# A four-layer kernel on one Trainium2 core: the value matmuls of the first attention in bursts of four units instead of two

## The chip, the cores and the metric

The kernel runs on one core of a Trainium2 chip. A core has TensorE (PE, with its weight loads PEld), VectorE (DVE), ScalarE (ACT), GpSimd (POOL) and SyncE (SP, which issues DMAs), each with its own instruction stream, tied by semaphores. The metric is the device time of one execution in microseconds, lower is better.

## What is computed

Four layers in sequence, each followed by a layer norm over the residual sum. The change lies in the first, an attention over two sequences of 2048 tokens with 16 heads of 16 columns; a decay multiplies the scores before the softmax. The other three are a feed-forward layer with weights and inputs rounded to a 4-bit grid, a causal linear attention, and a mixture of eight experts.

```python
def _L0_attn_ref(x, Wq, bq, Wk, bk, Wv, bv, Wo, bo, alpha):
    ...
    scores = jnp.einsum('bqhd,bkhd->bhqk', q, k) * scale
    idx = jnp.arange(T)
    lag = jnp.abs(idx[:, None] - idx[None, :]).astype(jnp.float32)
    decay = jnp.exp(-alpha * lag * DT)
    scores = scores * decay
    attn = jax.nn.softmax(scores, axis=-1)
    out = jnp.einsum('bhqk,bkhd->bqhd', attn, v).reshape(B, T, D)
    return out @ Wo.T + bo
```

## The kernel before

The first attention works on 16 pairs of heads in sequence. For each pair there are two kinds of work.

The **units**. A unit is one block of 128 keys against 512 queries, for both heads of the pair; a query block has 16 units (TB) and a pair has four query blocks, so 64 units (UNITS). PE makes the unit's scores (line 823, two matmuls, 512 columns) into one of two PSUM buffers `ps_s`. ACT makes the exponentials from there into `prob` (line 969), a ring of RING units in SBUF. Four of the 16 units of a query block are diagonal ("d" in SCORE_ORDER): ACT copies their scores to `tb` (line 959), POOL multiplies them by the decay (line 927) and subtracts the row's maximum (line 930), and ACT takes the exponential from `tb` (line 966), four to nine units later, as EXP_ORDER says. In the last pair DVE does POOL's part (lines 883 and 887). The values (line 839) multiply `prob` by V into `ps_o`: four groups of 32 columns of the array work side by side, and each matmul shows as two records in the trace, so a unit has eight records. Each query block sums in its own half of `ps_o`; behind its last unit ACT copies the half to `ot` (line 946), PE transposes it (line 846) and DVE divides (lines 904 and 906): a "sum".

The **tiles**. For the pair after this one, 128 tiles of approximate scores (line 799, one matmul of 512 columns each) give the rows' maxima. PE writes a tile into one of three PSUM banks of the ring `ps_r` (BANKS), and DVE multiplies it by the decay and takes its maximum (line 870, two records: the pass and the reading of the accumulator, which releases the bank). The sums and the turn of the maxima take a slot in the same ring. Once per pair DVE folds the maxima (line 891), PE transposes them (line 804), and DVE splits them into three parts (lines 331 to 339): the "turn".

The order on PE is written out by `body_steps`, and DVE follows the same list: two units, each with its two tiles around it, then the values of the two units that lie LAG = 4 units back, then the next two units. EARLY shifts the tiles three ahead, so three of them stand in a row where a pair begins. ACT has its own loop over the exponentials (EXP_ORDER), with the copies to `tb` in front of some and the copy of the last query block's sums behind the second exponential of each query block. The semaphores that matter: `ring_free` (DVE has read a bank; PE waits for the user of the same bank, three slots earlier as a rule), `exp` and `copied` (a score buffer is free; PE waits for the score two before), `value` (the values of a unit are done; ACT waits for the unit RING before, and the copy out for the whole block), `evac` (the sums are copied; PE waits before it begins the next block but one in that half).

Of the kernel before, what the change touches and what calls it, by code (L numbers as in the profile page):

```python
# [19 lines left out]
TB = T // P  # L20
# [75 lines left out]
def up_to(n):  # L96

    return n + 1
# [32 lines left out]
UNITS = QB * TB  # L131
# [4 lines left out]
TURN = 3  # L136
BANKS = 3
EARLY = 3
RING = 6
LAG = 4  # L140
EXP0, PV0, EV0 = TB, 5, 1

# [19 lines left out]
def e_unit(u):  # L164
    return unit(EXP_ORDER, u)


def place_in(order, u, other):

    qb, n = divmod(u, TB)  # L170
    nth = order[:n].count(order[n])
    return qb * TB + [i for i, c in enumerate(other) if c == order[n]][nth]


def diag_count(u):

    qb, n = divmod(u, TB)
    return qb * TPC + SCORE_ORDER[:n].count("d")


def body_kind(this, nxt):

    if not this:
        return "first"
    if not this.back():
        return "lead"
    return "last" if not nxt else "mid" if nxt.more() else "late"


@lru_cache(None)  # L190
def body_steps(kind):

    fold, turn = [("fold", None, 1)], [("turn", None, 1)]
    if kind == "first":
        small = [("tile", t, 1) for t in range(TILES)] + fold + [("tile", t, 2) for t in range(TURN)] + turn
        small += [("tile", t, 2) for t in range(TURN, SKEW)]
        steps, slot = [], 0
        for what, n, ahead in small:  # L200
            steps.append((what, n, slot if what != "fold" else None, ahead))
            slot += what != "fold"
        return steps
    small = []
    if kind != "last":
        small = [("tile", t, 1) for t in range(SKEW, TILES)] + fold
        if kind in ("lead", "mid"):
            small += [("tile", t, 2) for t in range(TURN)] + turn + [("tile", t, 2) for t in range(TURN, SKEW)]
        else:
            small += turn  # L210
    steps, done, slot = [], 0, 0
    def next_small(upto):
        nonlocal done, slot
        while done < min(len(small), upto):
            what, n, ahead = small[done]
            steps.append((what, n, slot if what != "fold" else None, ahead))
            done, slot = done + 1, slot + (what != "fold")

    for two in range(0, UNITS + (LAG if kind == "last" else 0), 2):
        for u in (two, two + 1):  # L220
            next_small(EARLY + 2 * u)
            if u < UNITS:
                steps.append(("score", u, None, 0))
            next_small(EARLY + 2 * u + 1)
        if two >= LAG:
            steps.append(("values", two - LAG, None, 0))
        elif kind != "lead":
            steps.append(("values", UNITS + two - LAG, None, -1))
        if two % TB == TB // 2 and (two > TB or kind != "lead"):
            steps.append(("sum", two // TB - 1 if two > TB else QB - 1, slot, 0 if two > TB else -1))  # L230
            slot += 1
    assert done == len(small)
    if kind == "last":
        steps.append(("sum", QB - 1, slot, 0))
    return steps


def slot_of(kind, what, n, ahead=None):

    return next(slot for w, m, slot, far in body_steps(kind) if (w, m) == (what, n) and ahead in (None, far))  # L240


@lru_cache(None)
def ring_use(kind):


    users = [-3, -2, -1]
    if kind == "last":
        past = ring_use("late")
        for i, (bank, _) in enumerate(past):  # L250
            users[bank] = i - len(past)
    out, bank = [], 1 if kind == "first" else 0
    for what, n, slot, _ in body_steps(kind):
        if slot is None:
            continue
        if kind != "lead" and what == "sum" and n in (0, QB - 1):
            bank = (bank + 1) % BANKS
        out.append((bank, slot - users[bank]))
        users[bank] = slot
        bank = (bank + 1) % BANKS  # L260
    if kind in ("first", "lead", "mid"):
        assert [b for b, _ in out[-3:]] == [0, 1, 2]
    return out
# [420 lines left out]
def stage_attention(nc, g, a, p1, p2, vp0, mx):  # L684
    with ExitStack() as ctx:
# [4 lines left out]
        mb = ctx.enter_context(nc.sbuf_tensor("mb", [P, 2, 2, T], F32))  # L690
        prob = ctx.enter_context(nc.sbuf_tensor("prob", [P, RING, 2, CH], F32))
        tb = ctx.enter_context(nc.sbuf_tensor("tb", [P, DIAGS, 2, CH], F32))
# [10 lines left out]
        def walk(body):  # L703

            def run(eng):
                body(eng, None, Pair(0, 0))
                for c in range(PAIRS - 1):
                    body(eng, Pair(0, c), Pair(0, c + 1))
                body(eng, Pair(0, PAIRS - 1), None)
            return run  # L710

        def first_slot(this):
            if not this:
                return 0
            if not this.back():
                return FIRST
            return this.times(SLOTS) + (FIRST - 1 if this.more() else FIRST - 1 - SKEW)

        with nc.Block() as block:
# [63 lines left out]
            def _(pe):  # L783
                def body(_, this, nxt):
                    if this is None:
                        return
                    for kind, n, slot, ahead in body_steps(body_kind(this, nxt)):
# [38 lines left out]
                        elif kind == "values":  # L826
# [6 lines left out]
                            for m in (n, n + 1):  # L833
                                qb, kb, _ = e_unit(m)
                                for f in range(2):
                                    for hh in range(2):
                                        q = 2 * f + hh
                                        out = ps_o[32 * q:32 * q + VW, qb % 2, :]
                                        mm = pe.matmul(out.rearrange("p (j c) -> p j c", c=P), vp[whose.par][:, kb, hh, :],  # L839
                                                       prob[:, m % RING, hh, :].rearrange("p (j f c) -> p f j c", f=2, c=P)[:, f],  # L840
                                                       start=(m % TB == 0), stop=(m % TB == TB - 1), skip_group_check=True)
# [93 lines left out]
            @block.scalar  # L935
            def _(act):
                def body(_, this, nxt):
                    if this is None:
                        return
                    slots = {n + QB * far: slot for k, n, slot, far in body_steps(body_kind(this, nxt)) if k == "sum"}  # L940

                    def evacuate(qb):
                        act.wait_ge(s["value"], up_to(this.times(UNITS) + (qb + 1) * TB + PV0))

                        act.wait_ge(s["ring_full"], up_to(first_slot(this) + (slots[qb - 1] + 1 if qb - 1 in slots else 0)))
                        act.activation(ot[:], ps_o[:, qb % 2, :], ACT.Copy).then_inc(s["evac"], 1)

                    e_diags = [n for n in range(UNITS) if e_unit(n)[2]]
                    for n in range(UNITS):
                        qb, kb, diag = e_unit(n)  # L950
                        if not diag:
                            mine = place_in(EXP_ORDER, n, SCORE_ORDER)
                            if SCORE_ORDER[(mine - 1) % TB] == "d" and nxt:

                                k = diag_count(mine - 1)
                                act.wait_ge(s["score"], up_to(this.times(UNITS) + mine))

                                act.wait_ge(s["exp"], up_to(this.times(UNITS) + place_in(SCORE_ORDER, mine - 1, EXP_ORDER) - TB + 1 + EXP0))
                                act.activation(tb[:, k % DIAGS], ps_s[:, (mine - 1) % 2], ACT.Copy).then_inc(s["copied"], 1)  # L959

                        last = UNITS % RING if n < UNITS % RING else RING
                        act.wait_ge(s["value"], up_to(this.times(UNITS) + n - last + 1 + PV0))
                        if diag:
                            k = e_diags.index(n)
                            act.wait_ge(s["less"], up_to(this.times(TB) + k + 1))
                            act.activation(prob[:, n % RING], tb[:, k % DIAGS], ACT.Exp).then_inc(s["exp"], 1)  # L966
                        else:
                            act.wait_ge(s["score"], up_to(this.times(UNITS) + mine + 1))
                            act.activation(prob[:, n % RING], ps_s[:, mine % 2], ACT.Exp,  # L969
                                           scale=csc[:, qb * TB + kb:qb * TB + kb + 1]).then_inc(s["exp"], 1)  # L970
                        if n % TB == 1 and (n > TB or this.back()):
                            evacuate(n // TB - 1)
                    if not nxt:
                        evacuate(QB - 1)

                walk(body)(act)


# [1606 lines left out]
```

## Time and profile before

| | |
|---|---|
| median of 3 runs | 3417.16 us (3413.48 to 3422.5) |
| the profiled execution, its own time | 3417.1 us |
| its span, first to last instruction | 3415.3 us |
| mean granted TensorE clock | 0.95 |
| busy, share of the span | PE 90%, PEld 51%, DVE 71%, ACT 53%, POOL 42% |
| records of L839 (values) | 8192, from 291.3 to 1785.7 us |
| records of L799 (tiles), attention alone | 1894 |

The first attention runs from about 290 to 1788 us. What is ahead of it is its projections, and what is behind it the other three layers. Busy shares are averages over stages with different limits, so for this change the rows of the attention alone are to be read.

### The profile page before, as it was taken

The numbers are of one execution on the slowest core, as the hardware profiler recorded it, in microseconds if no ns is written. First come the engines' busy times: TensorE is split into PE (matmuls) and PEld (weight loads), VectorE is DVE, ScalarE is ACT, GpSimd is POOL, SyncE is SP. The second block draws the span as 40 slices with busy tenths as digits, with TensorE's granted clock in tenths as the row PEclk, the third lists the DMA queues.
The fourth block names the chain that finished last, engine by engine and source line by source line (L and its number), as shares of the span: only waits on it lengthen the run. The fifth ranks groups of instructions, "written<-read, shape, count | busy, mean of one in ns | idle before, by whom it ended". The sixth has DMA issues, their size and how long they took to land. (4 is left out here: it accounts for less than half of the span.)

```text
span 3415.3 us, 66017 instructions
## 1 busy us (share of the span) xinstructions
PE 3071.1 (90%) x22948; PEld 1734.7 (51%) x22949; DVE 2440.1 (71%) x6509; ACT 1802.2 (53%) x2255; POOL 1422.7 (42%) x741
## 2 busy tenths in 40 slices
PE   3678999999999999999985998989999987999996
PEld 1232333333333333333323565556666666999995
DVE  4679999999999999999747888844555554333334
ACT  4235888888888888888873333322222222111112
POOL 6346787878878787787801000000000111111110
PEclk7788999999999999999997999989899988999998
DMA  5575434332344443333204110030000005555555
GB/s 154 144 192 138 90 84 83 79 78 76 67 91 92 93 89 82 83 79 78 57 13 78 25 38 5 1 99 14 14 14 14 23 18 191 183 182 177 182 184 182
DMA packets 201698, 304.65 MB, mean 89 GB/s; under 512 B 86192, under 2 KB 150544, under 8 KB 199248
## 3 DMA queue, kind: packets, MB, share of 16 engines
q1 hardware_dynamic: 192640, 277.89, 31.6%
q0 software_dynamic: 7632, 22.16, 1.8%
q8 instruction: 159, 2.61, 0.3%
q14 instruction: 115, 0.94, 0.1%
q10 hardware_dynamic: 1152, 1.05, 0.1%
HBM read 238.91 MB, written 62.13 MB: 88 GB/s over the span
## 5 line engine op out<-in xcount | busy, mean ns | idle before, releaser
L870 DVE CUSTOM_DVE_ANT_0 ps_r<-ps_r,toep 128x512 f32<-128x512 f32 x1894 | 1252.3, 716 | 71.8 <-PE ps_r L799 31.6
L969 ACT ACTIVATE prob<-ps_s,csc 128x1024 f32<-128x1024 f32 x768 | 829.9, 1118 | 151.4 <-PE ps_s L823 129.6
L927 POOL TENSOR_TENSOR tb<-tb,toep 128x1024 f32<-128x1024 f32 x240 | 568.1, 2367 | 264.0 <-ACT tb L959 229.4
L799 PE MATMUL ps_r<-p 96*128 96x512 bf16 x1894 | 646.3, 382 | 10.1 <-DVE mp L870 4.1
L823 PE MATMUL ps_s<-p 120*128 120x512 bf16 (+1 forms) x2048 | 609.3, 380 | 27.1 <-ACT tb L959 16.4
L930 POOL TENSOR_TENSOR tb<-tb,mb 128x1024 f32<-128x1024 f32 x240 | 567.8, 2366 | 18.8
L839 PE MATMUL ps_o<-prob,vp 128*32 128x256 f32 x8192 | 548.2, 385 | 1.2 <-ACT prob L966 0.9
L799 PEld LDWEIGHTS ps_r<-p 96*128 96x128 bf16 x1894 | 181.4, 96 | 406.2 <-DVE mp L870 258.0
L1695 POOL DMA_INDIRECT slots_scratch<-l_xh,l_place x64 | 62.5, 976 | 710.3 <-DVE l_xh L2020 693.3
L839 PEld LDWEIGHTS ps_o<-prob,vp 128*32 128x32 f32 x8192 | 213.7, 109 | 269.6 <-issue 177.9
L823 PEld LDWEIGHTS ps_s<-p 120*128 120x128 bf16 (+1 forms) x2048 | 189.6, 98 | 237.2 <-ACT tb L959 46.6
L2335 ACT ACTIVATE e_aT<-e_u 128x1024 f32<-128x1024 f32 x71 | 75.0, 1057 | 421.4 <-DVE e_u L2406 421.4
L966 ACT ACTIVATE prob<-tb 128x1024 f32<-128x1024 f32 x256 | 272.3, 1064 | 2.9 <-POOL tb L930 2.8
L2281 PEld LDWEIGHTS ps_eu<-e_hT,moe_w 128*128 128x128 f32 x2272 | 266.3, 193 | 7.7 <-DVE e_hT L2397 4.1
L2281 PE MATMUL ps_eu<-e_hT,moe_w 128*128 128x128 f32 x2272 | 266.9, 276 | 3.5 <-DVE e_hT L2397 3.5
L870 DVE DVE_READ_ACCUMULATOR2_ANT mp<- 128x1 f32 x1894 | 266.2, 141 | 0.0
L959 ACT ACTIVATE tb<-ps_s 128x1024 f32<-128x1024 f32 x240 | 247.0, 1029 | 32.7 <-PE ps_s L823 31.3
L2374 POOL DMA_INDIRECT ytok_scratch<-e_y,e_name x71 | 69.2, 975 | 463.0 <-DVE e_y L2452 463.0
L2299 PE MATMUL ps_ed<-moe_w,e_aT 128*128 x1136 | 257.0, 379 | 0.8 <-DVE e_y L2452 0.8
L2406 DVE TENSOR_TENSOR e_u<-ps_eu,moe_cols 128x1024 f32<-128x1024 f32 x71 | 86.9, 1224 | 210.1 <-PE ps_eu L2281 210.1
L2299 PEld LDWEIGHTS ps_ed<-moe_w,e_aT 128*128 128x128 f32 x1136 | 210.3, 190 | 26.9 <-issue 1.2
L1280 PE MATMUL ps_du<-wgu,d_xs 128*128 128x512 f32 (+1 forms) x384 | 164.6, 580 | 4.2 <-DVE d_h L1559 2.6
(324 smaller groups left out, 3580.4 us busy)
## 6 DMA issues: line engine op xcount, KB each, us to landing
moe_w<-in_W_dram SPq DMA_DIRECT2D x79, 1024.0 KB, 5.3
p<-scr_scratch SPq DMA_DIRECT2D x288, 192.0 KB
mb<-mrow_scratch SPq DMA_DIRECT2D x16, 2048.0 KB, 7.4
scr_scratch<-part SPq DMA_DIRECT2D x64, 384.0 KB, 6.7
p<-scr_scratch SPq DMA_DIRECT2D x96, 128.0 KB
moe_pt<-slots_scratch SPq DMA_DIRECT2D x72, 132.0 KB, 2.1
vscr_scratch<-vsb SPq DMA_DIRECT2D x8, 1024.0 KB, 8.8
vp<-vscr_scratch SPq DMA_DIRECT2D x16, 512.0 KB, 22.2
```

The lines of the kernel that those rows point to most:

```text
L799: pe.matmul(ps_r[:, bank, :], buf[:, hh, 0, qt * P:(qt + 1) * P], buf[:, hh, 1, kc * CH:(kc + 1) * CH], start=True, stop=True)\
L823: mm = pe.matmul(ps_s[:, n % 2, hh, :], buf[0:rows, hh, KEY, kb * P:(kb + 1) * P], buf[0:rows, hh, var, qb * CH:(qb + 1) * CH], start=True ...
L839: mm = pe.matmul(out.rearrange("p (j c) -> p j c", c=P), vp[whose.par][:, kb, hh, :], prob[:, m % RING, hh, :].rearrange("p (j f c) -> p f ...
L870: dve.tensor_tensor_reduce(ps_r[:, bank, :], ps_r[:, bank, :], toep[:, col:col + CH], 1.0, -3.0e38, ALU.mult, ALU.max, mp[:, whose.par, hh ...
L927: pool.tensor_tensor(tb[:, k % DIAGS], tb[:, k % DIAGS], toep[:, col:col + CH].unsqueeze(1) .broadcast_to([P, 2, CH]), ALU.mult).then_inc( ...
L930: pool.tensor_tensor(tb[:, k % DIAGS], tb[:, k % DIAGS], mb[:, this.par, :, qb * CH:(qb + 1) * CH], ALU.add).then_inc(s["less"], 1)
L959: act.activation(tb[:, k % DIAGS], ps_s[:, (mine - 1) % 2], ACT.Copy).then_inc(s["copied"], 1)
L966: act.activation(prob[:, n % RING], tb[:, k % DIAGS], ACT.Exp).then_inc(s["exp"], 1)
L969: act.activation(prob[:, n % RING], ps_s[:, mine % 2], ACT.Exp, scale=csc[:, qb * TB + kb:qb * TB + kb + 1]).then_inc(s["exp"], 1)
L1280: mm = pe.matmul(ps_u[:, lo:hi], xs[:, c % 2, kc, t * P:(t + 1) * P], wgu[:, kc, lo:hi], start=(kc == 0), stop=(kc == KC - 1), skip_group_ ...
L2281: mm = pe.matmul(ps_u[:, tile.par, f, :], w1[:, tile.par, kc, f * P:(f + 1) * P], hT[:, kc, :], start=(kc == 0), stop=(kc == KC - 1), skip ...
L2299: mm = pe.matmul(ps_d[:, 0:D], aT[:, this.par, f, :], w["w2"][:, bass.ds(e, 1), f, :].rearrange("p a n -> p (a n)"), start=(f == 0), stop= ...
```

## The change

RING goes from 6 to 8 units. The values no longer come two units at a time behind every second score but four units at a time behind every fourth: behind scores 2 and 3 of each four (of the step with `two` = 2, 6, 10, ...) PE works off the units `two` - 6 to `two` - 3. The oldest two units are so read two units later than before, and the younger two at the same place. ACT copies a block's sums out behind the fourth exponential of the next block, not the second. PV0, a count of units ahead of the first one, follows RING.

```diff
-RING = 6
+RING = 8
 LAG = 4
-EXP0, PV0, EV0 = TB, 5, 1
+BURST = 4
+EXP0, PV0, EV0 = TB, RING - 1, 1
...
-        if two >= LAG:
-            steps.append(("values", two - LAG, None, 0))
-        elif kind != "lead":
-            steps.append(("values", UNITS + two - LAG, None, -1))
+        if (two - LAG) % BURST == BURST - 2 and (two >= LAG or kind != "lead"):
+            for n in range(two - LAG - BURST + 2, two - LAG + 2, 2):
+                steps.append(("values", n % UNITS, None, 0 if n >= 0 else -1))
         if two % TB == TB // 2 and (two > TB or kind != "lead"):
...
-                        if n % TB == 1 and (n > TB or this.back()):
+                        if n % TB == BURST - 1 and (n > TB or this.back()):
                             evacuate(n // TB - 1)
```

On PE, four units in the middle of a pair: `ps_r` are the tiles, `ps_s` the scores (two instructions each), `ps_o` the values, whose 8 instructions are two units and 16 records of the trace. Before:

```order
L839 MATMUL ps_o<-prob,vp 32x256 x8
L799 MATMUL ps_r<-p_0 128x512
L823 MATMUL ps_s<-p_1 128x512 x2
L799 MATMUL ps_r<-p_0 128x512 x2
L823 MATMUL ps_s<-p_1 128x512 x2
L799 MATMUL ps_r<-p_0 128x512
L839 MATMUL ps_o<-prob,vp 32x256 x8
```

and now:

```order
L839 MATMUL ps_o<-prob,vp 32x256 x16
L799 MATMUL ps_r<-p_0 128x512
L823 MATMUL ps_s<-p_1 128x512 x2
L799 MATMUL ps_r<-p_0 128x512 x2
L823 MATMUL ps_s<-p_1 128x512 x2
L799 MATMUL ps_r<-p_0 128x512 x2
L823 MATMUL ps_s<-p_1 128x512 x2
L799 MATMUL ps_r<-p_0 128x512 x2
L823 MATMUL ps_s<-p_1 128x512 x2
L799 MATMUL ps_r<-p_0 128x512
L839 MATMUL ps_o<-prob,vp 32x256 x16
```

Four tiles stood between two bursts, now eight do, and a burst is twice as long.

On ACT, where a query block begins: L959 copies diagonal scores, L969 and L966 are exponentials, L946 copies the last block's sums out. Before:

```order
L946 ACTIVATE ot<-ps_o 128x256
L959 ACTIVATE tb<-ps_s 128x1024
L969 ACTIVATE prob<-ps_s,csc 128x1024 x2
L966 ACTIVATE prob<-tb 128x1024
L969 ACTIVATE prob<-ps_s,csc 128x1024
```

and now:

```order
L959 ACTIVATE tb<-ps_s 128x1024
L969 ACTIVATE prob<-ps_s,csc 128x1024 x2
L946 ACTIVATE ot<-ps_o 128x256
L966 ACTIVATE prob<-tb 128x1024
L969 ACTIVATE prob<-ps_s,csc 128x1024
```

The copy out has moved behind a copy of scores and two exponentials. DVE, POOL and SP have the same instructions in the same order as before; the waits that count units of the ring moved with it.

## Rows read from the trace of the kernel before

**Rows 1.** The page: the span, and each engine's busy us, share and instructions.

```profile
span 3415.3 us, 66017 instructions
...
PE 3071.1 (90%) x22948; PEld 1734.7 (51%) x22949; DVE 2440.1 (71%) x6509; ACT 1802.2 (53%) x2255; POOL 1422.7 (42%) x741
```

**Rows 2.** Stretch table, and line 804's group (ns min/median/max, first and last start).

```profile
core 0: us, PE busy (x) PEld busy (x) DVE busy (x) ACT busy (x) POOL busy (x), PEclk, DMA share, GB/s
360.30:1689.40 1329.10, 1307.87 (x10861) 504.06 (x10857) 1254.59 (x3776) 1139.50 (x1176) 1057.85 (x448) 1.00 0.37 82
...
1689.40:1788.00 98.60, 84.81 (x823) 28.49 (x823) 43.41 (x49) 85.10 (x88) 17.37 (x8) 1.00 0.09 27
...
L804 PE MATMUL ps_r<-ident,nm x15: 269/285/286, 360.3 to 1689.4; 128*32 128x128 f32 x15
```

**Rows 3.** Timeline of PE, one ordinary step: start us, us, engine, line, names, count.

```profile
1017.34 0.39 PE L799 MATMUL ps_r<-p 96*128 96x512 bf16 x1
...
1018.43 0.60 PE L823 MATMUL ps_s<-p 120*128 120x512 bf16 x2
1018.86 0.38 PE L799 MATMUL ps_r<-p 96*128 96x512 bf16 x1
1019.17 1.07 PE L839 MATMUL ps_o<-prob,vp 128*32 128x256 f32 x16
1020.18 0.39 PE L799 MATMUL ps_r<-p 96*128 96x512 bf16 x1
```

**Rows 4.** Timeline of DVE in the same step.

```profile
1017.91 0.70 DVE L870 CUSTOM_DVE_ANT_0 ps_r<-ps_r,toep 128x512 f32<-128x512 f32 x1
...
1020.48 0.14 DVE L870 DVE_READ_ACCUMULATOR2_ANT mp<- 128x1 f32 x1
1020.76 0.70 DVE L870 CUSTOM_DVE_ANT_0 ps_r<-ps_r,toep 128x512 f32<-128x512 f32 x1
```

**Rows 5.** Timeline of PE and DVE where a pair of heads starts.

```profile
1043.37 0.89 PE L799 MATMUL ps_r<-p 96*128 96x512 bf16 x3
...
1043.94 0.70 DVE L870 CUSTOM_DVE_ANT_0 ps_r<-ps_r,toep 128x512 f32<-128x512 f32 x1
...
1045.21 0.73 DVE L870 CUSTOM_DVE_ANT_0 ps_r<-ps_r,toep 128x512 f32<-128x512 f32 x1
...
1045.86 0.14 DVE L870 DVE_READ_ACCUMULATOR2_ANT mp<- 128x1 f32 x1
...
1046.07 0.38 PE L799 MATMUL ps_r<-p 96*128 96x512 bf16 x1
...
1046.38 1.07 PE L839 MATMUL ps_o<-prob,vp 128*32 128x256 f32 x16
...
1047.38 0.39 PE L799 MATMUL ps_r<-p 96*128 96x512 bf16 x1
```

**Rows 6.** Timeline of PE, its window cut inside a burst.

```profile
309.70 0.64 PE L839 MATMUL ps_o<-prob,vp 128*32 128x256 f32 x8
```

**Rows 7.** Timeline of DVE round a sum.

```profile
1011.02 0.73 DVE L870 CUSTOM_DVE_ANT_0 ps_r<-ps_r,toep 128x512 f32<-128x512 f32 x1
...
1012.37 0.69 DVE L870 CUSTOM_DVE_ANT_0 ps_r<-ps_r,toep 128x512 f32<-128x512 f32 x1
```

**Rows 8.** Timeline of DVE, the turn of the maxima.

```profile
1025.95 0.28 DVE L331 COPY mt<-ps_r 32x128 f32<-32x128 f32 x1
...
1027.31 0.68 DVE L870 CUSTOM_DVE_ANT_0 ps_r<-ps_r,toep 128x512 f32<-128x512 f32 x1
```

**Rows 9.** Timeline of ACT, exponentials in a row.

```profile
1018.37 2.12 ACT L969 ACTIVATE prob<-ps_s,csc 128x1024 f32<-128x1024 f32 x2
1020.36 1.07 ACT L966 ACTIVATE prob<-tb 128x1024 f32<-128x1024 f32 x1
```

**Rows 10.** Who waited for whom, 360 to 1690 us: total us, times, longest.

```profile
ACT ot L946 <- PE ps_o L839: 52.5, 56, 0.9
...
PE ps_s L823 <- ACT tb L959: 14.4, 56, 0.3
```

## The prediction

> **What bounds the kernel now.** I read the page first, then the stretch table, the timeline of PE and of DVE in one ordinary step, the waits, and last a place where the order differs. The span is 3415.3 us with PE busy 90% of it [rows 1]. The change touches the first attention alone. Its fifteen turns of the maxima (one per pair that has a successor) start from 360.3 to 1689.4 us, so one pair of heads takes 1329.1 / 14 = 94.94 us; over those fourteen pairs PE is busy 98% at full granted clock, DVE 94%, ACT 86% and POOL 80% [rows 2]. Three engines are nearly full, so the reader should distrust "PE is the bound" and ask which loop closes last.
>
> In an ordinary step of two units PE goes from the tile behind one burst to the tile behind the next in 1020.18 - 1017.34 = 2.84 us: 1.52 us to its fourth tile, 0.31 from there to the burst, 1.01 for the burst of 16 records [rows 3]. The seven matmuls up to the fourth tile take 0.217 each, eight take 1.74, so one burst and its two borders cost 1.10 on top.
>
> DVE in the same step reads four tiles from 1017.91, is ready for the next at 1020.48, 0.64 a tile (0.65 back to back, 1045.21 to 1045.86 [rows 5]; I use 0.645), and starts the next at 1020.76: idle 0.28 per step [rows 4]. It began on the first tile 0.57 behind that tile's matmul start (1017.34).
>
> Now the loop. Tiles go through three PSUM banks, so a tile's matmul needs the read of the tile three slots earlier. Where each pair of heads starts, three tiles stand in a row behind a burst and six lie between two bursts. There the timeline shows the ring closing: first tile 1043.37, DVE on it at 1043.94 (0.57), on the third at 1045.21 (two tiles, 1.27), its maximum read out from 1045.86, the sixth tile's matmul at 1046.07 (0.86 behind the third's start), the burst 0.31 later, the next first tile at 1047.38 (1.00) [rows 5]. The sum is 0.57 + 1.27 + 0.86 + 0.31 + 1.00 = 4.01, exactly what this step takes. So a step with n ring slots takes, by the ring, 2.74 + 0.645 (n - 4): at n = 4 that is 2.74, only 0.10 under PE's own 2.84. PE bounds the ordinary step by a tenth of a microsecond, and the ring bounds every longer one.
>
> **The change part by part.**
>
> *Bursts merged.* Between bursts there are now four units and eight slots. PE's own time for four units was 5.68. One entry and one exit fall away: two bursts with borders cost 2 x (0.31 + 1.00) = 2.62; one burst of 32 records costs 0.31 + 0.86 + 1.00 = 2.17, since another 16 records are four more waves of four at 0.215. (A window that ends inside a burst shows the waves: 8 records 0.64 [rows 6], 16 records 1.07 [rows 3], so two waves add 0.43.) One ordinary border of 0.215 comes in its place. PE alone: 5.68 - 2.62 + 2.17 + 0.22 = 5.45, a gain of 0.23 per four units. The first row of a longer burst is missing; bounds: 0.74 for the second half, by the start pace inside a burst (0.69 over 15 gaps, 0.046 x 16), and 1.00, as if nothing were saved. I take 0.86, which the wave rows give.
>
> *The ring under a longer burst.* The eighth tile stands right before the burst and needs the bank of the fifth. By the loop: 0.57 + 4 x 0.645 + 0.86 + 2.17 = 6.18 us, against 5.68 now and against PE's 5.45. Put from DVE's side: at the burst it has three tiles in hand, 1.94 us of work less the 0.21 it has begun; the burst and the way to the next reading last 2.17 + 0.57 = 2.74. It idles about 1.0 us per four units instead of 0.56. PE then waits about 0.7 us at the ring before it. Nothing in the change deepens this ring (BANKS stays 3; the ring that grows is the one of probabilities). The release of a bank costs 0.86 [rows 5], and reads as 0.95 in the ordinary step [rows 3, 4] (1017.91 to 1018.86, where PE's order came last); the first is the wait itself, the second my upper bound.
>
> The Trainium skill, page "TensorEngine Tiling (Array Packing)", section Key Properties, says that changing the tiling mode drains the engine. The entry of 0.31 against 0.215 agrees with it. By that rule alone the change gains 0.23 per four units, the PE rival below. The same page, section Performance Considerations, says that tiling speeds up TensorE but not the emptying of PSUM, which may become the limit; DVE reading PSUM at 0.645 a tile is that limit here [rows 4].
>
> *Counting a pair.* Of the sixteen stretches between bursts nine are ordinary: 55.6. Four hold a sum, for which DVE needs 1012.37 - 1011.02 = 1.35 from one tile to the next instead of 0.65 [rows 7]: 4 x 6.88 = 27.5. The one at the pair's start has ten slots: 7.47. The one with the fold has seven slots and a reduction (between nothing and one tile, I take 0.45): 6.0. The one with the turn has DVE's chain of 1025.95 to 1027.31, 1.36 [rows 8], in a slot that reaches DVE sooner than a tile does: 6.7, within 0.3. Sum 103.3, against 94.94: +8.35 a pair.
> Fourteen pairs: +117. Pair 0 has twelve such stretches before its turn, at 8.35 / 16 = 0.52: +6.
>
> *Behind the last turn* (98.6 us, no tiles) ACT is busiest, 85.1 [rows 2]. Two score buffers let a score start only when the exponential two before is done. Per four units: two exponentials 2.0 [rows 9], 0.1 to the score, 0.43 for it, burst 0.10 + 1.86, next score 0.70: 5.2, and some 19 such stretches fit in 98.6 today at 5.2. Between 0 and +8; I take +4.
>
> *Ring of eight.* The probabilities of unit n + 8 need the values of unit n. The score of n + 8 is the first behind the burst that reads n, so the bank order already keeps this wait: no cost. It takes away ACT's wait for values; that wait stands in the trace only in the copies out, next. DVE, POOL and SP run the same instructions. SP waits for two more units' values before it loads the next V, early in a pair of 94.94 us.
>
> *Sums copied behind the fourth exponential.* Now ACT waits 52.5 us in 56 copies, 0.94 each, for the burst, and PE waits for the scores copied behind it 14.4 us in 56, one such wait in each block of sixteen units, 0.26 at its matmuls [rows 10]. Moved, the copy finds its burst done. That is worth at least 1.0 a pair; my count of 103.3 has no such wait in it, so it is already spent. If the wait stayed, the count would be 1.0 too low, well inside the range. Is ACT hurt by the longer burst? Two exponentials in a row take 1.99 to the next start [rows 9]. From the end of the score behind a burst to the end of the one behind the next, the chain is: two exponentials 2.0 and a hand-over 0.1, the seventh score 0.43, the burst's borders and body 0.31 + 1.86, a tile 0.22, the score 0.60, a hand-over 0.1: 5.6, under 6.18 and so covered. If the ring were not there, this 5.6 and not PE's 5.45 would bound.
>
> *Sum.* 3417.1 (the profiled execution, whose time is the median of the runs, 3417.16) + 117 + 6 + 4 = **3544 us**.
>
> **The rivals.**
> - *Ring binds, as summed:* 0.78. Its own range: second half of the burst at 0.74 gives -0.12 in 236 stretches, -28, and -4 behind the last turn: 3512. At 1.00 +33, release at 0.95 +21, last turn +4: 3602.
> - *PE or ACT binds, the ring does not (faster):* DVE would have to keep its stock through the burst. Then ACT's 5.6 a stretch gives 16 x 5.6 = 89.6 a pair, -5.3 in 14.8 pairs, -79: 3338. For it: PE is 98% busy and the merged burst is really shorter; ACT's 0.94 wait really goes. Against: the step of 4.01 with six slots, where the same engine waits for the same banks. It decides from the point where the ring stretch falls under 5.93 (94.94 / 16), that is, if 32 records and their borders took under 1.92 and not 2.17. Chance 0.07.
> - *The ring binds, but by half:* part of the next tile's weight load or DVE's start lies under the burst, so that the mean stretch is only 0.15 to 0.4 over today's 5.93: 236 of them give 3452 to 3511. Chance 0.05.
> - *ACT and DVE take turns waiting (slower yet):* the seventh score stands behind the seventh tile at the ring, 3.6 us into the stretch; its score buffer is free at about 3.0. If ACT is over 0.6 late (a copy and two diagonal exponentials fall in one stretch of four), the late score pushes the eighth tile, some 0.5 to 1 us per block: 59 blocks, 3575 to 3610. Chance 0.08.
> - *Nothing measurable:* gain and loss cancel within 0.3%. Chance 0.02.
>
> 0.3% (about 10 us) is what a measurement tells from no change. The predicted time is the first case's. The range 3510 to 3592 leaves out the faster and the half case and the upper tail of the two slower ones, about 0.2. Faster 0.07, same 0.02, slower 0.91.
>
> **What the profile of the changed kernel would show.** Right: turns 103 us apart; L839 bursts of 32 records, last start about 1.55 behind the first; L799 behind it at 1.86; 0.57 to DVE; PE idle before L799 released by DVE, some 0.7 per four units, PE's share between the turns down from 98% to about 87% (its busy 93.4 a pair less 16 x 0.23, over 103.3); DVE idle 1.0 behind each burst, share down from 94% to 87%; ACT's wait in L946 gone. Wrong: turns nearer 90 us with DVE's gaps no longer than now; or PE waiting for ACT and not for DVE; or a burst whose first 16 and last 16 records lie apart. A slower granted clock than 1.00 between the turns would also break the sum.

## The result: slower by 3.6%, and the profile after

The changed kernel takes 3553.84 us (median of 4 runs, 3534.2 to 3561.26) against 3419.83 (4 runs, 3413.48 to 3437.29). The ratio is 1.036, 95% interval 1.031 to 1.040. The prediction was 3544, in 3510 to 3592.

The page of the changed kernel and its stretch table, between the first and the last turn of the maxima and behind the last turn; they answer to [rows 1] and [rows 2].

```profile
span 3545.5 us, 66017 instructions
...
PE 3090.7 (87%) x22948; PEld 1758.6 (50%) x22949; DVE 2424.7 (68%) x6509; ACT 1808.4 (51%) x2255; POOL 1420.2 (40%) x741
```

```profile
core 0: us, PE busy (x) PEld busy (x) DVE busy (x) ACT busy (x) POOL busy (x), PEclk, DMA share, GB/s
363.90:1805.50 1441.60, 1321.30 (x10846) 519.33 (x10843) 1238.34 (x3774) 1145.21 (x1175) 1054.71 (x448) 1.00 0.35 76
1805.50:1912.00 106.50, 83.32 (x839) 31.29 (x839) 43.42 (x49) 84.03 (x88) 17.07 (x8) 1.00 0.08 25
```

```profile
L804 PE MATMUL ps_r<-ident,nm x15: 269/284/287, 363.9 to 1805.5; 128*32 128x128 f32 x15
```

The turns now lie (1805.5 - 363.9) / 14 = 102.97 us apart, 94.94 before; fourteen times the difference is 112.5 of the 130.2 us by which the span grew. PE's share there fell from 98% to 92% and DVE's from 94% to 86%. DVE's busy time fell by 16 us and PE's rose by 13, with the same number of instructions; what grew on both is the waiting. (Why PE's busy time is no exact measure here stands under "Shares" below.) The granted clock is 1.00 before and after. The rest: pair 0 up to its turn +3.6 (of which 1.1 lies ahead of the first values), behind the last turn up to the last values +7.9 (1909.7 - 1805.5, against 1785.7 - 1689.4), and 6.2 in the three later layers. I don't put these last down to the change. In the kernels below, which don't touch those layers, they take 1623 to 1656 us in one profile each, while two kernels whose attention should be equal agree in the turns to 0.01 us (94.94 and 94.95, 93.63 twice). So I read the attention by the distance of the turns and the whole by the ratio.

One ordinary stretch of the changed kernel, from behind one burst to behind the next, PE and DVE mixed by time; it answers to [rows 3] and [rows 4].

```profile
1112.84 0.39 PE L799 MATMUL ps_r<-p 96*128 96x512 bf16 x1
...
1113.42 0.70 DVE L870 CUSTOM_DVE_ANT_0 ps_r<-ps_r,toep 128x512 f32<-128x512 f32 x1 [0.88 <-PE ps_r L799]
...
1115.98 0.73 DVE L870 CUSTOM_DVE_ANT_0 ps_r<-ps_r,toep 128x512 f32<-128x512 f32 x1
...
1116.18 0.39 PE L799 MATMUL ps_r<-p 96*128 96x512 bf16 x1 [0.26 <-DVE mp L870]
...
1116.84 0.38 PE L799 MATMUL ps_r<-p 96*128 96x512 bf16 x1
...
1117.15 1.93 PE L839 MATMUL ps_o<-prob,vp 128*32 128x256 f32 x32
...
1118.58 0.14 DVE L870 DVE_READ_ACCUMULATOR2_ANT mp<- 128x1 f32 x1
...
1119.02 0.39 PE L799 MATMUL ps_r<-p 96*128 96x512 bf16 x1
...
1119.60 0.70 DVE L870 CUSTOM_DVE_ANT_0 ps_r<-ps_r,toep 128x512 f32<-128x512 f32 x1 [0.88 <-PE ps_r L799]
```

This is the loop of the ring, term by term. First tile 1112.84, DVE on it 0.58 later. DVE begins the fifth tile 2.56 later, at 1115.98. The eighth tile, which needs the fifth's bank, starts 0.86 later at 1116.84. The burst starts 0.31 later and the next first tile 1.87 behind it, at 1119.02. Sum 6.18. The gap that the trace shows on PE's own matmuls stands one tile earlier: the seventh (1116.18, idle 0.26) waits for the fourth's bank, and from it a tile and a score, 0.22 + 0.43, lead to 1116.84 as well, because DVE's read takes the same 0.65. The ring closes at both, with the same sum.

DVE sits idle 0.88 us before the first tile behind a burst ("<-PE ps_r"), and the table of waits puts that at 185.6 us in 208 cases, where the kernel before had 25.8 in 56.

Who waited for whom, changed kernel, 360 to 1790 us (total us, times, longest); it answers to [rows 10].

```profile
PEld ps_r L799 <- DVE mp L870: 470.4, 1220, 0.9
...
ACT prob L969 <- PE ps_s L823: 276.2, 223, 2.0
DVE ps_r L870 <- PE ps_r L799: 185.6, 208, 1.2
PE ps_r L799 <- DVE mp L870: 63.4, 253, 0.5
```

PE's matmuls of tiles wait for DVE 253 times, and DVE waits for PE 185.6 us in 208 bursts. PE and DVE wait for each other in turn, which is what a ring too short for the burst looks like. ACT waits 276 us for scores. In return no matmul of PE is listed as waiting for ACT in this window, and only 18.3 us of its weight loads (9.7 + 6.3 + 2.3). The wait of the copy out [rows 10] has gone from the list.

### The profile page after: what moved, and what is told of

The parts are those of the page before. It is cut to its first block and busy times, and to the rows that moved or that the text cites. A ratio compares the mean times of both kernels' runs of the same rounds, so it can differ in the third digit from the quotient of the medians.

```text
span 3545.5 us, 66017 instructions
## 1 busy us (share of the span) xinstructions
PE 3090.7 (87%) x22948; PEld 1758.6 (50%) x22949; DVE 2424.7 (68%) x6509; ACT 1808.4 (51%) x2255; POOL 1420.2 (40%) x741
## 5 line engine op out<-in xcount | busy, mean ns | idle before, releaser
L969 ACT ACTIVATE prob<-ps_s,csc 128x1024 f32<-128x1024 f32 x768 | 827.0, 1114 | 311.3 <-PE ps_s L823 309.3
L799 PE MATMUL ps_r<-p 96*128 96x512 bf16 x1894 | 680.8, 384 | 99.1 <-DVE mp L870 67.1
L839 PE MATMUL ps_o<-prob,vp 128*32 128x256 f32 x8192 | 495.1, 382 | 0.6 <-ACT prob L966 0.6
L839 PEld LDWEIGHTS ps_o<-prob,vp 128*32 128x32 f32 x8192 | 239.9, 109 | 198.9 <-issue 53.1
L966 ACT ACTIVATE prob<-tb 128x1024 f32<-128x1024 f32 x256 | 271.7, 1061 | 2.7 <-POOL tb L930 2.7
L959 ACT ACTIVATE tb<-ps_s 128x1024 f32<-128x1024 f32 x240 | 246.9, 1029 | 48.0 <-PE ps_s L823 38.6
```

Of the source, the lines that this page charges most:

```text
L799: pe.matmul(ps_r[:, bank, :], buf[:, hh, 0, qt * P:(qt + 1) * P], buf[:, hh, 1, kc * CH:(kc + 1) * CH], start=True, stop=True)\
```

## The experiments

All distances between turns come from the first and last start of line 804's matmul, divided by 14; "last values" is the last start of a record of line 839, in each kernel's one profile. The ratios of the experiments are against executions of the kernel before from the same series (medians 3416 to 3423 us).

| kernel | turns apart, us | last values, us | median, us | ratio to before, 95% |
|---|---|---|---|---|
| before | 94.94 | 1785.7 | 3419.83 | |
| changed | 102.97 | 1909.7 | 3553.84 | 1.031 to 1.040 |
| short_read_burst4 | 95.16 | 1798.0 | 3434.04 | 1.001 to 1.006 |
| short_read_burst2 | 93.85 | 1770.6 | 3402.73 | 0.993 to 0.997 |
| score_first | 109.26 | 2003.1 | 3638.39 | 1.060 to 1.072 |
| short_score_first | 97.10 | 1822.7 | 3461.97 | 1.009 to 1.017 |
| burst4_copy2 | 102.99 | 1912.8 | 3558.49 | 1.034 to 1.043 |
| copy4_only | 99.38 | 1860.3 | 3491.53 | 1.017 to 1.028 |
| ring8_only | 94.95 | 1784.6 | 3420.79 | 0.996 to 1.002 |
| copy_between | 93.63 | 1766.3 | 3402.23 | 0.992 to 0.997 |
| ring8_between | 93.63 | 1765.5 | 3403.10 | 0.989 to 0.995 |
| ring8_between_early2 | 93.55 | 1766.9 | 3399.88 | 0.992 to 0.997 |

Theories: the **ring** (three PSUM banks of tiles don't last through a burst of 32 records); **ACT** (a longer time between scores starves the exponentials); **PE** (its own work, which got shorter); and for the moved copy, that it **costs** or **gives** time by itself.

**1. Cheaper reads by DVE, burst of four.** In both kernels of this pair three tiles in four are read over 256 of their 512 columns; the maxima leave those keys out, and everything else is computed.

```diff
-                            dve.tensor_tensor_reduce(ps_r[:, bank, :], ps_r[:, bank, :], toep[:, col:col + CH],
+                            wide = CH if kc == qt // TPC else CH // 2
+                            dve.tensor_tensor_reduce(ps_r[:, bank, 0:wide], ps_r[:, bank, 0:wide], toep[:, col:col + wide],
...
```

> The changed kernel, but DVE reads only 256 of the 512 columns of three tiles in four (so the maxima leave those keys out; matmuls, exponentials and values are all there). If the ring of three banks under the long burst is what made the change slower, a cheaper read shortens the loop from 6.18 us to about 0.57 + 4 x 0.45 + 0.75 + 2.17 = 5.3 us, under PE's own 5.45 and ACT's chain of 5.6: pairs 88 to 91 us apart, the time 3330 to 3370 us, faster than the kernel before. If the long burst slows the kernel by itself, or by ACT's starved exponentials, the stretch stays near 6.1 us and the time within 30 us of the changed kernel's 3550.

Measured: 3434 us, 120 less than the changed kernel, turns 95.16 apart. PE's and ACT's work are the same, so 7.8 us a pair hang on how long DVE holds the banks. But it didn't get to 88 to 91: my expectation missed by 4 to 7 us a pair, and the kernel is not faster than the one before, as I had expected, but 0.3% slower. The timeline of PE and ACT in one of its stretches shows what comes next (lines from 870 on have moved down by one in this kernel):

```profile
1003.94 1.93 PE L839 MATMUL ps_o<-prob,vp 128*32 128x256 f32 x32
...
1006.04 0.60 PE L823 MATMUL ps_s<-p 120*128 120x512 bf16 x2
...
1006.73 2.12 ACT L970 ACTIVATE prob<-ps_s,csc 128x1024 f32<-128x1024 f32 x2 [1.67 <-PE ps_s L823]
...
1008.90 0.60 PE L823 MATMUL ps_s<-p 96*128 96x512 bf16 x2
...
1009.35 0.38 PE L799 MATMUL ps_r<-p 96*128 96x512 bf16 x1
...
1009.66 1.93 PE L839 MATMUL ps_o<-prob,vp 128*32 128x256 f32 x32
...
1011.52 0.39 PE L799 MATMUL ps_r<-p 96*128 96x512 bf16 x1
```

The score behind the burst starts at 1006.04, ACT takes it at 1006.73 and is done with two exponentials at 1008.85, and the fourth score, which needs the second one's buffer, starts at 1008.90. Then 0.45 to the tile, 0.31 to the burst, 1.86 to the next tile (1011.52) and 0.23 to the score: 0.69 + 2.17 + 0.45 + 0.31 + 1.86 + 0.23 = 5.71, this stretch to 0.01 (1009.66 - 1003.94 = 5.72). That is ACT's chain, which I had priced at 5.6. Other ordinary stretches take up to 5.79. Those with a sum still take 6.28 to 6.69, the one with the turn 6.06 and the one at a pair's start 6.23 to 6.44, and those I had not counted. So the ring is the first bound and ACT's chain the second, 0.46 below it; PE's 5.45 is not met in any ordinary stretch that I read.

**2. The same reads, burst of two.**

> The same cut of DVE's reading in the kernel before (bursts of two units; the maxima leave those keys out). By the ring theory PE bounds the ordinary step of 2.84 us already, so only the longer steps gain (the one of 4.01 at a pair's start falls to about 3.3): pairs about 94 us apart, 3400 to 3415 us. If DVE's share of 94% were the bound, pairs would fall under 90 us and the time under 3350.

Measured: 93.85 apart, 3402.7 us, inside the expected 3400 to 3415. Cheaper reads are worth 1.1 us a pair under bursts of two and 7.8 under bursts of four. With cheap reads on both sides the burst of four is still slower, 95.16 against 93.85. So DVE's cost explains 6.7 of the 8.03 us by which the turns moved apart, and 1.3 is left; I put that to ACT's chain and the stretches with a sum, which no run takes apart.

**3. The score first behind the burst.** The same PE work, one tile later.

```diff
-            next_small(EARLY + 2 * u)
+            next_small(EARLY + 2 * u - (u % BURST == 0 and u > 0))
```

> The changed kernel with one edit in the order: behind a burst the score comes first and then three tiles, in place of tile, score, two tiles. PE's work and its mode changes are the same. By the ring theory the first tile reaches DVE 0.43 us later and every stretch grows by that, 6.18 to 6.6 us: pairs about 109 to 110 us apart, some 3640 to 3655 us. By the theory that ACT's wait for the next score is what costs, the score comes 0.22 us sooner and the time falls by up to 50 us; by the theory that PE's own work bounds, nothing changes.

Measured: 109.26 apart, 3638 us. The turns are where I expected them, the time is 2 us below the expected 3640 to 3655. The ordinary stretches grow from 6.18 to 6.61, by the 0.43 that a score takes, and so do those with a sum (7.04 to 7.47). The stretch at a pair's start, which the edit leaves alone, stays at 7.47. Fifteen stretches of 0.42 on average are the 6.29 us by which the turns moved. ACT gets its score earlier and PE has the same to do; only the first tile's way to DVE is longer. This is the clearest test of the loop.

**4. Both edits, cheap reads and score first.**

> The changed kernel with the cheaper reads of DVE (keys left out of the maxima) and the score first behind the burst. With the cheap reads alone the stretches are 5.72 us, where PE waits for exponentials. If ACT's chain of score, two exponentials, score and burst is what bounds there, a score 0.22 us earlier takes up to 0.2 off the stretch: 5.5 to 5.6, pairs 92 to 94.5 us, 3385 to 3430 us. The same edit cost 85 us under the full reads. If the ring of banks were still the bound, the edit would cost again, 0.4 us a stretch, 3510 us or more.

Measured: 97.10 apart, 3462 us: slower than 95.16, so neither of the two outcomes that I had expected: not the gain that ACT's chain promised, nor the 0.4 us a stretch of a ring that binds throughout. The timeline of PE and DVE:

```profile
1002.57 1.93 PE L839 MATMUL ps_o<-prob,vp 128*32 128x256 f32 x32
...
1004.44 0.60 PE L823 MATMUL ps_s<-p 120*128 120x512 bf16 x2
...
1005.45 0.43 DVE L871 CUSTOM_DVE_ANT_0 ps_r<-ps_r,toep 128x256 f32<-128x256 f32 x1 [1.96 <-PE ps_r L799]
...
1006.00 0.39 PE L799 MATMUL ps_r<-p 96*128 96x512 bf16 x1
...
1006.65 0.39 PE L799 MATMUL ps_r<-p 96*128 96x512 bf16 x1 [0.26 <-DVE mp L871]
...
1008.49 1.93 PE L839 MATMUL ps_o<-prob,vp 128*32 128x256 f32 x32
```

The burst at 1002.57 leaves DVE idle 1.96 us, and it begins the first of three tiles at 1005.45. The fourth tile waits for the first one's bank (1006.00), the fifth for the second one's, a full read (1006.65, 0.26 idle); from there PE's own matmuls run to the burst at 1008.49. The burst lets the score start at 1004.44, the fifth tile comes 2.21 later and the next burst 1.84 behind that: in this stretch the loop closes through the fifth tile instead of the eighth, 1.87 + 2.21 + 1.84 = 5.92. The stretch that begins at 1014.40, with the full read on the third tile, takes 5.81, and there the last tile that is held up is the seventh, which needs the fourth's bank. I had asked only what stands before the burst. A ring shorter than what PE could send behind the burst binds there too.

**5. The copy out moved alone**, in the kernel before.

```diff
-                        if n % TB == 1 and (n > TB or this.back()):
+                        if n % TB == 3 and (n > TB or this.back()):
```

> The kernel before with only the copy of a block's sums moved behind the fourth exponential (bursts of two, ring of six). If that wait of 0.94 us is what delays the score behind it, one step in eight falls from 3.25 to 2.84 us: 1.6 us a pair, about 24 us in all, 3395 us. If the wait is covered elsewhere the time stays at 3418.

Measured: 99.38 apart, 3491.5 us, 2.3% slower where I expected 0.7% faster. PE and ACT where a block begins:

```profile
1010.98 0.38 PE L799 MATMUL ps_r<-p 96*128 96x512 bf16 x1
...
1012.38 0.39 ACT L946 ACTIVATE ot<-ps_o 128x256 f32<-128x256 f32 x1
...
1012.82 1.07 PE L839 MATMUL ps_o<-prob,vp 128*32 128x256 f32 x16 [1.46 <-ACT ot L946]
```

PE could start the first values of the new block at 1011.3, 0.31 behind its tile, and gets to start them at 1012.82, when ACT has copied out the block before. They wait for that copy although they go to the other half of `ps_o`: the wait ahead of line 839 counts the copies of all blocks up to the last one, and my sentence on `evac` ahead of the prediction ("the next block but one") was wrong. The new block's first values stand behind its sixth score under bursts of two and behind its eighth under bursts of four. So the copy can stand behind the fourth exponential without loss only together with the burst of four. Behind the last turn this kernel loses more: 106.9 us up to the last values against 96.3.

**6. The copy back behind the second exponential**, in the changed kernel.

```diff
-                        if n % TB == BURST - 1 and (n > TB or this.back()):
+                        if n % TB == 1 and (n > TB or this.back()):
```

> The changed kernel with only the copy of the block's sums put back behind the second exponential. ACT then waits in it for the burst behind the fourth score, about 2 us a block, and the copy of the fourth score behind it comes late, so the sixth score starts some 0.3 us late. By the ring theory PE has 0.73 us to spare in a stretch and DVE still has tiles, so it is covered: pairs 103 to 103.8 us apart, 3550 to 3562 us. By the theory that ACT's waits add to DVE's, each block loses a further 0.4 to 1.0 us: 3575 to 3610 us.

Measured: 102.99 apart against 102.97, 3558 us. ACT's copy out in its timeline:

```profile
1010.71 0.38 ACT L946 ACTIVATE ot<-ps_o 128x256 f32<-128x256 f32 x1 [2.23 <-PE ps_o L839]
```

ACT waits 2.23 us and the turns don't move. In the changed kernel the place of the copy is worth nothing up to the last turn, because the ring closes later. Behind the last turn, where no tiles are left, the old place costs 2.3 us (106.5 up to the last values against 104.2), which the medians can't tell from their spread.

**7. The ring of eight alone**, in the kernel before (`RING = 8`, `PV0` = 7).

> The kernel before with only the ring of probabilities at eight units. 64 units are no multiple of six, so at each pair's start the first exponential waits 1.3 us for values of the old pair; with eight it does not. The stretch there is bound by the ring of tiles (4.01 us), so I expect nothing from it: pairs 94.9, 3410 to 3420 us. If ACT's wait counts, up to 1.3 us in 14 pairs: 3399 us.

Measured: 94.95 apart, ratio 0.996 to 1.002. ACT's wait of 1.3 us at each pair's start is gone and the stretch there still takes 4.01 to 4.02. No cost and no gain.

**8. The copy where ACT would wait anyway**, bursts of two, ring of six.

```diff
+                        if n % TB == 2 and (n > TB or this.back()):
+                            evacuate(n // TB - 1)
                         last = UNITS % RING if n < UNITS % RING else RING
...
-                        if n % TB == 1 and (n > TB or this.back()):
-                            evacuate(n // TB - 1)
```

It stands behind the copy of the fourth score (line 959) and ahead of the third exponential.

> The kernel before (bursts of two, ring of six) with the copy of a block's sums between the copy of the fourth score and the third exponential. There ACT would wait for its next score anyway, the fourth score's buffer is free before, and the sums are copied before the next block's first values come. The 0.41 us that one step in eight loses should go and no new wait come: pairs 93.3 us apart, 24 us off, 3388 to 3398 us. If the copy still comes after PE reaches the next block's values, part of the 1.5 us of the run with the fourth exponential returns and the time is 3420 or more.

Measured: 93.63 apart, the last values at 1766.3 instead of 1785.7, ratio 0.992 to 0.997 over 12 runs.

```profile
L804 PE MATMUL ps_r<-ident,nm x15: 269/285/285, 359.2 to 1670.0; 128*32 128x128 f32 x15
```

```profile
PE ps_s L823 <- ACT tb L959: 0.6, 2, 0.3
```

The first row is the distance of the turns; the second, from the table of waits, answers to [rows 10]: PE's waits for copied scores are down from 14.4 us in 56 to 0.6 in 2. In the timeline three steps a pair fall from 3.25 to 2.84 us, but the one with the turn, also 3.25 before, only to 3.13; that is the 1.3 us a pair instead of the 1.6 that I expected. The attention is 19.4 us shorter; the median is 3402, above my 3388 to 3398, and the three layers behind vary by more than that difference. This version beats both kernels, by 0.6% and 4%.

**9. The same with the ring of eight.**

> The same with the ring of probabilities at eight. If the wait at a pair's start is covered by the ring of tiles, it is equal to the kernel with the copy between, within 5 us. If not, 5 to 18 us less.

Measured: 93.63 apart, the same. Its profiled execution spent 1649.8 us behind the last values against 1626.1, with a granted clock of 0.88 from 2200 to 3000 us where the kernel of run 8 had 0.93 and the kernel before 0.92. It and one more took 3417 and 3416 us at a mean clock of 0.94, the other four 3399 to 3404 at 0.946 to 0.949. So I put the difference to the later layers and not to the edit.

**10. And with a pair that starts with two tiles.**

```diff
-EARLY = 3
+EARLY = 2
...
-        while done < min(len(small), upto):
+        while done < len(small) and done - sum(w == "fold" for w, _, _ in small[:done + 1]) < upto:
```

> The kernel before with ring of eight and the copy between, and with the fold taking no tile's place in the order, so that a pair starts with two tiles in a row instead of three (EARLY 2). By the loop of the ring the stretch at a pair's start has five slots, 3.39 us and not 4.01, and a step near the fold gets its fourth tile back, 0.22: -0.4 us a pair, 3 to 8 us less than the same kernel without it. If PE's matmuls alone counted, nothing changes, since their number is the same.

Measured: 93.55 apart, ratio 0.992 to 0.997. The step at a pair's start fell from 4.02 to 3.37 (the loop said 3.39), but the step before the turn grew from 2.62 to 2.83 and the one of the turn from 3.13 to 3.44. That is 0.65 gained and 0.52 given back, 0.13; the mean over the pairs is 0.08, where I expected 0.4. (One step with a sum took 3.49 instead of 3.34, in one of the five pairs that I read.) The median is 3 us lower, within the spread of the later layers. Tiles can be moved between steps, but each step that is full pays for them.

## Why the prediction was right

- **What bounds.** Right. The loop, read from one odd step of the old trace (4.01 us with six slots), gave 6.18 us for a stretch that did not exist yet, and 6.18 was measured. Its terms: 0.57 became 0.58, 4 x 0.645 = 2.58 became 2.56, 0.86 stayed, 0.31 + 1.86 became 0.31 + 1.87. Runs 1 and 3 show that it is the cause: a cheaper read takes the loss away, and a later first tile adds its own 0.43, in every stretch that has it and in no other. The ring of eight and the copy's place, tried alone (runs 7, 5 and 6), leave the burst as the part that costs.
- **The burst.** Right. 32 records take 1.93 us and let the next tile start 1.86 to 1.87 behind their start. The two bounds of the unknown (0.74 and 1.00 for the second half) were not needed. DVE's gap behind it is 0.88 us, where I had said 1.0; the 0.14 between them is the accumulator's record of the last tile, which counts as busy.
- **Per pair.** 103.3 forecast, 102.97 measured, +8.35 against +8.03. The stretch at a pair's start 7.47 was 7.47; those with a sum 6.88 were 6.84 to 7.05; fold and turn together 12.7 were 5.57 + 6.59 = 12.16. The last was the term off, by the guess of 0.45 for the fold and a turn that hides more.
- **Pair 0 and behind the last turn.** +6 and +4 forecast, +3.6 and +7.9 measured. The second is under-sized, and not by its price: a block of 16 units of the last pair takes 20.75 us (bursts at 1843.45 and 1864.20), 5.19 per four units, against the 5.2 that I priced. What I had wrong is the kernel before, for which I took 5.2 as well; there a block takes 18.99 us (bursts at 1727.66 and 1746.65), 4.75 per four units. Four blocks at 1.76 are 7.0 of the 7.9. The timeline of PE and ACT shows the wait:

```profile
1850.22 1.04 PE L823 MATMUL ps_s<-p 120*128 120x512 bf16 x4
1850.93 2.12 ACT L969 ACTIVATE prob<-ps_s,csc 128x1024 f32<-128x1024 f32 x2 [1.87 <-PE ps_s L823]
...
1853.10 0.61 PE L823 MATMUL ps_s<-p 96*128 96x512 bf16 x2 [0.40 <-ACT prob L969]
...
1853.64 1.93 PE L839 MATMUL ps_o<-prob,vp 128*32 128x256 f32 x32
...
1855.51 1.04 PE L823 MATMUL ps_s<-p 120*128 120x512 bf16 x4
```

  0.71 + 2.17 + 0.54 + 1.87 = 5.29: score, two exponentials, score, burst, with no tile in it. Runs 1 and 3, which change only what concerns the tiles, take 104.2 and 104.3 us there, like the changed kernel.
- **Luck in the total.** By parts I forecast 117 + 6 + 4 + 0 = 127 and the profiles give 112.5 + 3.6 + 7.9 + 6.2 = 130.2. The forecast was 7 us too high up to the last turn and 4 too low behind it, and the later layers, which it put at nothing, happened to add 6.2. That the total came within 4 us of the profiled execution (3547.24; the median lies 7 above it) owes something to these three.
- **Shares.** DVE 86% (87 forecast), but PE 92%, where I had said 87%. A tile's record lasts 0.38 us and the next matmul may start 0.22 behind it, so a wait of up to 0.16 leaves no gap in the busy time. The loss must be read from starts, not from shares.
- **The ring of eight.** Right as to cost (run 7). Wrong in a side remark: ACT's wait for values stood in the trace at each pair's start too, 14 times 1.3 us, not only in the copies out. It was covered.
- **The copy behind the fourth exponential.** I wrote that it was worth at least 1.0 us a pair and already spent in the count. Spent, yes (run 6: the turns don't move). Its worth hangs on the place: alone it costs 4.4 us a pair (run 5), between copy and exponential it gives 1.3 (run 8).
- **The faster rival.** That PE binds was refuted by runs 1 to 3. My 3338 for it was too low as well: with the ring's loss mostly removed the kernel stood at 3434, since ACT's chain is 5.7 and not 5.6, and the stretches with a sum or a turn take 6.06 to 6.69.
- **The rule of the Trainium skill.** The Trainium skill, page "TensorEngine Tiling (Array Packing)", section Key Properties, says that changing the tiling mode drains the engine. The trace agrees as to a cost at each border: merging two bursts saves 2.62 - 2.17 - 0.22 = 0.23 us of PE time, and with the borders at 0.31 and 1.87 that was there after the change. It was saved on an engine that then waited 6.18 - 5.45 = 0.73 for DVE. The Trainium skill, same page, section Performance Considerations, says that tiling speeds up TensorE but not the emptying of PSUM, which may become the bottleneck. Here the emptying did decide, though not by its rate alone: DVE was busy 86% and idle 0.88 us behind a burst, because three banks don't last through it.

What stays open: a deeper ring of tiles under the burst of four was not tried, though it is the most direct test of the loop. The scores, the values and the tiles hold 4 + 1 + 3 units of 512 fp32 columns of PSUM in the kernel's own declarations, and a fourth tile bank would have to come out of the score buffers.

## What to carry to other kernels

Before two bursts on one engine are merged, count what the other engines have in hand when the burst begins: for the consumer not to run dry, ring depth times its time per item must cover the burst plus the way to the first new item (here 3 x 0.65 = 1.95 against 2.17 + 0.58 = 2.75). Look in the old trace for an odd step in which the order already strays from the pattern; it tells from measured times alone what the loop costs. A wait that shows in the table is worth moving only if the new place is one where the engine waits anyway and nobody needs the result sooner; try such a part alone, since here the part alone went 2.3% the wrong way and a place two exponentials earlier went 0.6% the right way.

## What the runs showed of the hardware

- In the column-tiled value matmuls every four records more add 0.215 us, however long the burst: 8 records 0.64 us [rows 6], 16 records 1.07 [rows 3], 32 records 1.93.
- The way into such a burst cost 0.31 us from the tile before (0.22 for an ordinary one) and the way out about 0.31 from the last record's start (1.55 behind the first of 32) to the next tile's; both the same for 16 and 32 records.
- A PSUM bank that DVE reads with an accumulated maximum was free for PE only 0.85 to 0.86 us after the read began, while the reads themselves follow each other at 0.65: the reading of the accumulator (0.14) and the hand-over come on top. The difference, 0.21, is a third of the 0.65 that a tile takes.
- Reading 256 instead of 512 columns took 0.38 us from one read to the next instead of 0.65 (run 4: 1006.45 to 1006.83).
